# The output weights' operands made during the query projections, kept in DRAM, and loaded by the attention into eleven places

## The chip, the cores and the metric

The kernel runs on one core of a Trainium2 chip. Its time is the device time of one execution in microseconds (us). The core has five engines that run side by side and wait for one another through semaphores: PE (TensorE, the matmuls), DVE (VectorE), ACT (ScalarE), POOL (GpSimd) and SP (SyncE, which here issues most of the DMAs). Transfers that SP issues go to the DMA queue that the profile calls q1, those that POOL issues to q0.

## What is computed

A transformer block on 4 sequences of 512 tokens, 1024 wide, float32:

```python
xn = layernorm(x)                                    # (4, 512, 1024)
qkv = xn @ w_qkv                                     # 32 query heads, 8 key/value heads, 128 each
scores = q @ k.T / sqrt(128) - slope[head] * sqrt(i - j)     # causal
attn = softmax(scores) @ v
attention = attn.reshape(4, 512, 4096) @ w_o         # w_o: (4096, 1024)
ffn = xn @ W.T + b + (the rank-r product A, B of the rank that a gate picks)
out = x + attention + ffn
```

Each float32 operand is split into a high part and the remainder, and each matmul is done as three (high by high, low by high, high by low): lines 677, 678 and 679 of the kernel before.

## The kernel before

**First phase, the projections, to about 1208 us.** Two pairs of sequences, one after the other, and for each seven 1024 x 1024 weight matrices in the order values, keys, FFN, Q0, Q1, Q2, Q3. A matrix is multiplied by Strassen's and Winograd's scheme in 2 x 2 blocks, in seven steps of 48 matmuls. For each step ACT makes the high part of a weight operand (`w_hi`, line 945, two halves of 128 x 1024) and DVE the low part (`w_lo`, line 1183); sums of weight blocks (lines 1260 to 1269) and of results (`res_a`, `res_b`, `res_hi`) are DVE's too. The step's matmuls can begin on a half when its low part is there. SP loads the weight blocks (`raw<-w_all`, 1 MB each); POOL issues the stores of the results to DRAM (`qk_s`, `v_s`).

**Second phase, the attention.** 128 units (a head of one sequence each), in 8 groups of 16 units. The head changes with every unit, the sequence every four, the pair of sequences every eight and the group every sixteen. For a unit PE makes the scores (`ps<-k,q`), DVE adds the bias and finds the row maxima (`neg_max`, line 1432), ACT takes exponentials, DVE inverts the row sums (`row_inv`, line 1443, once per unit), PE transposes the probabilities (`ps<-ident,probs`, line 877), ACT and DVE split them (`pt_hi`, `pt_lo`), and PE multiplies by v.

Between these pieces PE does the output projection in "fills" (`ps<-wo,op_hi` and the like): a set of four units is multiplied by its rows of w_o, again in seven Strassen steps, for two tiles of tokens, 14 fills in a set. The set 4g is the first of group g. Its fills run in units 6 to 9 of the group, steps 0 to 3 of the first tile in unit 6 and steps 4 to 6 in unit 7. A fill's result is added to `acc` by DVE (line 1467); `acc` tiles come from and go to DRAM (`acc_s`), moved by SP.

**The operands of w_o.** Each group needs the seven Strassen operands of its own 512 rows of w_o, each as a high and a low part of 128 x 1024. Before, they are made inside the attention: SP loads four blocks `wo_raw` (line 448, 512 KB each; for a later group in unit 10 of the one before), POOL makes the four sums (`wo_sums`, line 657, in 16 pieces), ACT the seven high parts and DVE the seven low parts (`out_split`; `wo<-wo_raw` and `wo<-wo_sum` in the trace). Tables of unit numbers (WO_SUMS_IN, HIGHS_IN, LOWS_EARLY, LOWS_LAST) put all of that into units 2 to 6 of each group of 16, for the first group too; the results lie in 9 places taken in turn. In DVE's program the low parts stand after a unit's last `acc` additions, ahead of the next unit's maxima.

**SP's order at the start of the attention.** SP works through units: for unit n it issues k, q and v as needed, then the w_o loads (units 1 and 2 for the first group), then `acc` transfers. All of this is one list: a transfer that has to wait holds back those behind it.

## Time and profile before

| | us |
|---|---|
| timed, median of 3 runs | 2472.9 (2472.09 to 2473.75) |
| the profiled execution | 2475.28 |
| its span in the profile | 2473.4 |
| PE busy in the span | 2377.9 (96%) |
| DVE, ACT, POOL busy | 1547.1, 1373.4, 784.2 |
| mean granted TensorE clock | 0.991 of full speed |

Times inside the execution are counted from the start of the span. A row of the timeline gives start, duration, engine, line, operation, output<-inputs and, in brackets, how long the engine had stood idle before it and what released it. Matmuls are pipelined, so that a single one's duration is longer than the distance to the next; starts are what to read.

### The profile page before, as it was taken

How to read it: one execution, taken by the hardware profiler on the slowest of the kernel's cores; microseconds unless marked ns; L12 is line 12 of the kernel's file. 1: busy time of each engine (PE TensorE's matmuls, PEld its weight loads, DVE VectorE, ACT ScalarE, POOL GpSimd, SP SyncE). 2: the span in 40 equal slices, each digit the busy share in tenths (PEclk: the TensorE clock that was granted, in tenths of full speed). 3: DMA queues.
4: the chain of work that ended last, by engine and by line, in shares of the span. 5: the costliest groups of instructions: out<-in, count | busy, mean ns of one | idle time of the engine just before them, and what ended most of it. 6: DMA issues, size and time to landing. Idle time of an engine off the chain costs nothing.

```text
span 2473.4 us, 34303 instructions
## 1 busy us (share of the span) xinstructions
PE 2377.9 (96%) x11616; PEld 1991.7 (81%) x11616; DVE 1547.1 (63%) x2969; ACT 1373.4 (56%) x3051; POOL 784.2 (32%) x1029
## 2 busy tenths in 40 slices
PE   5999999998799999999899999999999999999999
PEld 4787888887678788888778888788888888888887
DVE  5657355655655645555676666767667666676665
ACT  4532133334533223333477777777777777777774
POOL 3211000000330100000244645446455464554644
PEclk9999999999899999999999999999999999999999
DMA  4536445546254635445655565655655556666553
GB/s 151 182 129 209 146 146 184 191 170 236 71 175 157 207 120 204 153 170 196 235 185 182 188 230 203 208 194 188 226 201 210 198 188 218 201 211 206 187 175 141
DMA packets 118318, 455.90 MB, mean 184 GB/s; under 512 B 11945, under 2 KB 12089, under 8 KB 109184
## 3 DMA queue, kind: packets, MB, share of 16 engines
q1 hardware_dynamic: 86176, 334.37, 39.2%
q0 software_dynamic: 31968, 119.33, 13.9%
q8 instruction: 94, 1.54, 0.2%
q14 instruction: 80, 0.66, 0.1%
HBM read 276.96 MB, written 176.69 MB: 183 GB/s over the span
## 4 chain that ended last, share of the span: by engine, by line
PE 85%; DVE 5%; ACT 4%; issue 3%; DMA 3%; POOL 1%; SPq 0%; ACTq 0%; DVEq 0%; POOLq 0%
PE ps L677 26%; PE ps L678 26%; PE ps L679 26%; PE ps L877 5%; DMA lora_lo<-lora_s 1%; DMA qk_s<-res_b 1%; ACT probs L1085 1%; ACT res_hi L945 1%; DVE stats L1197 1%; DVE wo L1183 1%; ACT rows L974 1%; PE ps L857 1%; ACT probs L1107 1%; DVE w_lo L1183 0%; DMA qk_s<-res_hi 0%
## 5 line engine op out<-in xcount | busy, mean ns | idle before, releaser
L945 ACT ACTIVATE w_hi<-raw 128x1024 fp32r<-128x1024 f32 x196 | 207.0, 1059 | 558.9 <-PE ps L679 439.5
L1467 DVE TENSOR_TENSOR acc<-ps,acc 128x512 f32<-128x512 f32 x448 | 297.2, 686 | 287.3 <-issue 260.8
L1183 DVE TENSOR_TENSOR w_lo<-raw,w_hi 128x1024 fp32r<-128x1024 f32 x196 | 239.1, 1224 | 357.8 <-ACT w_hi L945 357.6
L677 PE MATMUL ps<-x_hi,w_hi 128*128 128x512 f32 x1120 | 436.5, 390 | 0.0
L678 PE MATMUL ps<-x_lo,w_hi 128*128 128x512 f32 x1120 | 436.0, 389 | 0.0
L679 PE MATMUL ps<-x_hi,w_lo 128*128 128x512 f32 x1120 | 435.9, 389 | 0.0
L1085 ACT ACTIVATE probs<-probs,neg_max 128x512 f32<-128x512 f32 (+3 forms) x512 | 283.9, 566 | 168.8 <-DVE neg_max L1432 168.8
L677 PE MATMUL ps<-wo,op_hi 128*128 128x512 f32 x896 | 363.5, 406 | 2.0 <-POOL op_lo L635 0.7
L678 PE MATMUL ps<-wo,op_hi 128*128 128x512 f32 x896 | 352.1, 393 | 0.0
L679 PE MATMUL ps<-wo,op_lo 128*128 128x512 f32 x896 | 351.5, 392 | 0.0
L679 PEld LDWEIGHTS ps<-x_hi,w_lo 128*128 128x128 f32 x1120 | 210.4, 188 | 43.9
L678 PEld LDWEIGHTS ps<-x_lo,w_hi 128*128 128x128 f32 x1120 | 210.4, 188 | 43.7
L677 PEld LDWEIGHTS ps<-x_hi,w_hi 128*128 128x128 f32 x1120 | 210.5, 188 | 43.1
L561 POOL DMA_DIRECT2D qk_s<-res_hi x40 | 30.1, 753 | 652.5 <-ACT res_hi L945 634.5
L1107 ACT ACTIVATE probs<-probs,row_inv 128x128 f32<-128x128 f32 x488 | 234.3, 557 | 1.1
L1183 DVE TENSOR_TENSOR pt_lo<-ps,pt_hi 128x512 fp32r<-128x512 f32 (+1 forms) x384 | 206.8, 593 | 28.9 <-ACT pt_hi L945 28.5
L945 ACT ACTIVATE pt_hi<-ps 128x512 fp32r<-128x512 f32 (+1 forms) x384 | 173.8, 526 | 76.6 <-PE ps L877 76.6
L635 POOL TENSOR_TENSOR op_lo<-at_raw,op_hi 128x256 fp32r<-128x256 f32 x192 | 142.6, 757 | 227.6 <-ACT op_hi L945 227.6
L635 POOL TENSOR_TENSOR op_lo<-op_raw,op_hi 128x256 fp32r<-128x256 f32 x192 | 143.0, 761 | 216.9 <-ACT op_hi L945 216.3
L1432 DVE CUSTOM_DVE_ANT_0 probs<-ps,bias 128x512 f32<-128x512 f32 (+2 forms) x384 | 202.1, 551 | 3.9 <-PE ps L679 1.0
L677 PEld LDWEIGHTS ps<-wo,op_hi 128*128 128x128 f32 x896 | 169.2, 189 | 36.7 <-issue 7.8
L679 PEld LDWEIGHTS ps<-wo,op_lo 128*128 128x128 f32 x896 | 168.6, 188 | 37.4
(166 smaller groups left out, 4637.1 us busy)
## 6 DMA issues: line engine op xcount, KB each, us to landing
raw<-w_all SPq DMA_DIRECT2D x70, 1024.0 KB, 5.4
q<-qk_s SPq DMA_DIRECT2D x128, 512.0 KB, 3.9
acc<-acc_s SPq DMA_DIRECT2D x128, 512.0 KB, 5.1
acc_s<-acc SPq DMA_DIRECT2D x112, 512.0 KB, 7.7
qk_s<-res_hi POOLq DMA_DIRECT2D x40, 1024.0 KB, 4.6
qk_s<-res_a POOLq DMA_DIRECT2D x20, 1024.0 KB, 9.2
qk_s<-res_b POOLq DMA_DIRECT2D x20, 1024.0 KB, 5.2
k<-qk_s SPq DMA_DIRECT2D x32, 512.0 KB, 3.6
```

Of the source, the lines that this page charges most:

```text
L561: pool.dma_start(qk_s[b, first:first + 4, :, level, :].rearrange("h p c -> p h c"), source).then_inc(signal, 16)
L635: nc.gpsimd.tensor_tensor(op_lo[part % STEPS][:, :, :], op_source(s, part), op_hi[:, part % STEPS].bitcast(F32), ALU.subtract).then_inc(s_ ...
L677: pe.matmul(to, st_hi, mv_hi, start=start, stop=False, skip_group_check=True)
L678: pe.matmul(to, st_hi, mv_lo, start=False, stop=False, skip_group_check=True)
L679: return pe.matmul(to, st_lo, mv_hi, start=False, stop=stop, skip_group_check=True)
L877: last = pe.transpose(to[:, c * P:(c + 1) * P], probs[:, n % 2, OFF[i] + j * P:OFF[i] + (j + 1) * P], ident[:, :])
L945: nc.scalar.activation(to, source, ACT.Copy).then_inc(signal, 1)
L1085: nc.scalar.activation(tile, tile, ACT.Exp, bias=neg_max[:, i:i + 1], scale=-1.0, accum_out=row_sum[:, i:i + 1]).then_inc(s_exp, 1)
L1107: last = nc.scalar.activation(tile, tile, ACT.Copy, scale=row_inv[:, i:i + 1])
L1183: nc.vector.tensor_tensor(to, source, high.bitcast(F32), ALU.subtract).then_inc(signal, 1)
L1432: nc.vector.tensor_tensor_reduce(out=to, in0=score_bank[i], in1=added, scale=-SCALE, scalar=3e38, op0=ALU.add, op1=ALU.min, accum_out=neg_ ...
L1467: nc.vector.tensor_tensor(to, fill[f % 2][:, :], to, ALU.add).then_inc(s_acc, 1)
```

## The change

All operands of w_o are made in the first phase and written to a new DRAM tensor `wo_s`. The work is cut into 32 quarters (8 groups, each 256 of the 1024 columns) of seven operands: 224 jobs of 128 x 256, 112 in the four query matrices of each pair. A job is a high part on ACT, a low part on DVE and a store by SP of both (256 KB, in 1-KB rows) from one of four slots `wp`. The four sums of a quarter are made on DVE behind its third job. SP loads a quarter as four blocks of 128 KB. STEP_JOBS gives the number of jobs in the seven steps of a query matrix (LAST_JOBS those of Q3): half of a step's jobs stand ahead of the second half of the next weight operand on ACT and DVE, half at the step's end. ACT's high part waits until the slot's store before last use has landed. SP's stores stand in its list among the weight loads, in the order in which DVE makes them.

In the attention nothing is made. SP loads finished operands, 1 MB each in 8-KB rows, into 11 places: for group 0, steps 0 to 3 in unit 1 and 4 to 6 in unit 2; for later groups steps 0 to 3 in units 10 to 13 of the group before and steps 4 to 6 in unit 6 of its own. PE waits for the load where it waited for the low part. The `bias` tile moves by 10 KB. POOL's `wo_sums`, the tables and the making are gone.

```diff
+QUARTERS = 4 * KV_HEADS
+JOBS = QUARTERS * STEPS
+WO_ORDER = (6, 1, 0, 4, 2, 5, 3)
+STEP_JOBS = (3, 5, 4, 5, 5, 4, 4)
+LAST_JOBS = (3, 5, 4, 5, 4, 2, 0)
+SLOTS = 4
+WO_PLACES = 11
...
+            def quarter(c, i):
+                group, part = c // 4, c % 4
+                head = group * G + 2 * (i % 2) + part // 2
+                first = (i // 2) * 512 + (part % 2) * 256
+                sp.dma_start(wp_raw[i][:, :], w_o[bass.ds(head * P, P), first:first + 256]).then_inc(s_wp_raw[i], 16)
+
+            def operands_out(pr, m, st, part_=None):
+                if m == Q0 and st == 0:
+                    sp.wait_ge(s_bank, 4 * (number(pr, FFN, STEPS - 1) + 1))
+                    for i in range(4):
+                        quarter(pr * QUARTERS // PAIRS, i)
+                for j in jobs(pr, m, st, part_):
+                    c, i = j // STEPS, j % STEPS
+                    part = slice(c % 4 * 256, (c % 4 + 1) * 256)
+                    sp.wait_ge(s_wp_lo, j + 1)
+                    sp.dma_start(wo_s[c // 4, WO_ORDER[i], :, :, part], wp[:, j % SLOTS].bitcast(F32)
+                                 ).then_inc(s_wp_out[j % SLOTS], 16)
+                    if i >= 3 and (c + 1) % (QUARTERS // PAIRS):
+                        sp.wait_ge(s_wp_sum, 4 * (c + 1))
+                        quarter(c + 1, {3: 2, 4: 3, 5: 1, 6: 0}[i])
...
+            def out_operand(group, step):
+                if used(group, step) is not None:
+                    sp.wait_ge(s_fill, used(group, step))
+                sp.dma_start(wo[wo_place(group, step)][:, :, :].bitcast(F32), wo_s[group, step]).then_inc(s_wo[step], 16)
 
             def out_weights(n):
                 if n in (1, 2):
-                    sp.wait_ge(s_bank, 4 * TOTAL)
-                    for i in ((0, 2), (1, 3))[n - 1]:
-                        out_block(0, i)
...
+                    if n == 1:
+                        sp.wait_ge(s_bank, 4 * TOTAL)
+                        operands_are_out(JOBS)
+                    for step in (range(0, 4), range(4, STEPS))[n - 1]:
+                        out_operand(0, step)
+                group, since = n // GROUP_UNITS, n % GROUP_UNITS
+                if since == 6 and group:
+                    for step in range(4, STEPS):
+                        out_operand(group, step)
+                if since in range(10, 14) and group + 1 < GROUPS:
+                    out_operand(group + 1, since - 10)
...
+            def job(j):
+                c, step = j // STEPS, WO_ORDER[j % STEPS]
+                if j >= SLOTS:
+                    act.wait_ge(s_wp_out[j % SLOTS], 16 * (j // SLOTS))
...
+                high(wp[:, j % SLOTS, 0], wp_source(step), s_wp_hi)
...
+            def job(j):
+                c, i = j // STEPS, j % STEPS
+                dve.wait_ge(s_wp_hi, j + 1)
...
+                low(wp[:, j % SLOTS, 1], wp_source(WO_ORDER[i]), wp[:, j % SLOTS, 0], s_wp_lo)
+                if i != 2:
+                    return
...
+                nc.vector.tensor_tensor(a21, a11, a21, ALU.subtract).then_inc(s_wp_sum, 1)
...
                         later_operand(pr, m, st, 1)
+                        for j in jobs(pr, m, st, 0):
+                            job(j)
                         weights(n + 1, 1)
...
                         ahead(pr, m, st)
+                        for j in jobs(pr, m, st, 1):
+                            job(j)
...
-                for part in making(n, LOWS_EARLY):
-                    out_split(*part)
...
-                for part in making(n, LOWS_LAST):
-                    out_split(*part)
```

How the order of instructions changes at three places. First DVE's list in unit 4 of a group (the first group change), before; `wo` is a low part of an operand, `acc` the addition of a fill, the ISA rows are the maxima of the next unit:

```order
L1443 RECIPROCAL row_inv<-row_sum 128x4
L1467 TENSOR_TENSOR acc<-ps,acc 128x512 x3
L1183 TENSOR_TENSOR wo<-wo_raw_93,wo 128x1024
L1183 TENSOR_TENSOR wo<-wo_raw_96,wo 128x1024
L1432 ISA probs,neg_max<-ps,bias 128x512
```

The same place after:

```order
L1463 RECIPROCAL row_inv<-row_sum 128x4
L1487 TENSOR_TENSOR acc<-ps,acc 128x512 x3
L1452 ISA probs,neg_max<-ps,bias 128x512
L1452 ISA neg_max 128x1
L1452 ISA probs,neg_max<-ps,bias 128x384
```

The two low parts between the last addition and the next maxima are gone; so are those of units 2, 5 and 6. Second, SP's list at the start of the attention, before, from the load of unit 1's q to that of unit 4's:

```order
L513 DMA q<-qk_s 128x1024
L448 DMA wo_raw_93<-w_o 128x2x512
L448 DMA wo_raw_95<-w_o 128x2x512
L513 DMA q<-qk_s 128x1024
L448 DMA wo_raw_94<-w_o 128x2x512
L448 DMA wo_raw_96<-w_o 128x2x512
L513 DMA q<-qk_s 128x1024
L474 DMA acc<-acc_s 128x1024 x2
L512 DMA k<-qk_s 128x1024
L513 DMA q<-qk_s 128x1024
```

And after:

```order
L554 DMA q<-qk_s 128x1024
L489 DMA wo_107<-wo_s 128x2048
L489 DMA wo_108<-wo_s 128x2048
L489 DMA wo_109<-wo_s 128x2048
L489 DMA wo_110<-wo_s 128x2048
L554 DMA q<-qk_s 128x1024
L489 DMA wo_111<-wo_s 128x2048
L489 DMA wo_112<-wo_s 128x2048
L489 DMA wo_113<-wo_s 128x2048
L554 DMA q<-qk_s 128x1024
L515 DMA acc<-acc_s 128x1024 x2
```

Ahead of unit 2's q stand four transfers of 1 MB where two of 512 KB stood, and three more of 1 MB ahead of unit 3's. Third, DVE's list where the matrix Q1 of the first pair ends and Q2 begins, before; `res_b` are the results of Q1's last step, lines 1260 to 1265 the sums of weight blocks for Q2:

```order
L1183 TENSOR_TENSOR res_b<-ps,res_hi 128x512 x4
L1183 TENSOR_TENSOR w_lo<-raw_55,w_hi 128x1024
L1260 TENSOR_TENSOR raw_57<-raw_56,raw_57 128x2048
L1262 TENSOR_TENSOR raw_56<-raw_54,raw_56 128x2048
L1265 TENSOR_TENSOR raw_54<-raw_57,raw_54 128x2048
L1183 TENSOR_TENSOR w_lo<-raw_54,w_hi 128x1024
```

And after, where `wp` is the low part of a job:

```order
L1203 TENSOR_TENSOR res_b<-ps,res_hi 128x512 x4
L1203 TENSOR_TENSOR wp<-wp_raw_78,wp 128x256
L1203 TENSOR_TENSOR wp<-wp_raw_76,wp 128x256
L1203 TENSOR_TENSOR w_lo<-raw_55,w_hi 128x1024
L1280 TENSOR_TENSOR raw_57<-raw_56,raw_57 128x2048
L1282 TENSOR_TENSOR raw_56<-raw_54,raw_56 128x2048
L1285 TENSOR_TENSOR raw_54<-raw_57,raw_54 128x2048
L1203 TENSOR_TENSOR wp<-wp_raw_75,wp 128x256
L1203 TENSOR_TENSOR w_lo<-raw_54,w_hi 128x1024
```

Two jobs stand ahead of the first weight half and one ahead of the second. Where Q0 ends and Q1 begins it is two jobs with a quarter's four sums between them.

## Rows read from the trace of the kernel before

**Rows 1.** Page, part 4: what the chain that ended last consists of, by engine.

```profile
PE 85%; DVE 5%; ACT 4%; issue 3%; DMA 3%; POOL 1%; SPq 0%; ACTq 0%; DVEq 0%; POOLq 0%
```

**Rows 2.** Windows: length, busy us (instructions) by engine, PEclk, DMA share, GB/s.

```profile
378.00:454.00 76.00, 76.00 (x337) 62.94 (x336) 42.31 (x37) 27.94 (x33) 6.03 (x8) 1.00 0.51 179
...
1352.00:1508.00 156.00, 153.34 (x816) 130.84 (x815) 106.01 (x275) 118.17 (x318) 78.14 (x104) 0.99 0.59 202
...
1215.00:1220.00 5.00, 4.39 (x17) 4.10 (x17) 3.84 (x13) 1.02 (x4) 1.11 (x2) 0.52 1.03 411
```

**Rows 3.** Timeline of DVE: the inverted row sums of units 16, 32, 48, 56 and 64.

```profile
1352.02 0.18 DVE L1443 RECIPROCAL row_inv<-row_sum 128x4 f32<-128x4 f32 x1 [0.60 <-ACT probs L1085]
...
1508.49 0.18 DVE L1443 RECIPROCAL row_inv<-row_sum 128x4 f32<-128x4 f32 x1 [0.60 <-ACT probs L1085]
...
1663.77 0.18 DVE L1443 RECIPROCAL row_inv<-row_sum 128x4 f32<-128x4 f32 x1 [0.60 <-ACT probs L1085]
...
1743.40 0.18 DVE L1443 RECIPROCAL row_inv<-row_sum 128x4 f32<-128x4 f32 x1 [0.60 <-ACT probs L1085]
...
1819.03 0.18 DVE L1443 RECIPROCAL row_inv<-row_sum 128x4 f32<-128x4 f32 x1 [0.61 <-ACT probs L1085]
```

**Rows 4.** Timeline of DVE in unit 4 of the fourth group.

```profile
1707.03 0.69 DVE L1467 TENSOR_TENSOR acc<-ps,acc 128x512 f32<-128x512 f32 x1 [3.68 <-issue]
1707.64 3.45 DVE L1183 TENSOR_TENSOR wo<-wo_raw,wo 128x1024 fp32r<-128x1024 f32 x2
1711.01 0.68 DVE L1432 CUSTOM_DVE_ANT_0 probs<-ps,bias 128x512 f32<-128x512 f32 x1
```

**Rows 5.** What PE waited for, 1250 us to the end: us, times, longest.

```profile
PE ps L877 <- DVE neg_max L1432: 19.1, 15, 1.8
```

**Rows 6.** Timeline of SP at the start of the attention: issues.

```profile
1208.07 0.90 SPq L448 DMA_DIRECT2D wo_raw<-w_o  x2
...
1210.83 0.47 SPq L513 DMA_DIRECT2D q<-qk_s  x1
...
1226.10 0.43 SPq L513 DMA_DIRECT2D q<-qk_s  x1
```

**Rows 7.** Timeline of PE: the first matmul of the scores of units 2, 3, 4 and 7.

```profile
1215.61 0.80 PE L677 MATMUL ps<-k,q 128*128 128x512 f32 x1 [3.13 <-DMA q<-qk_s]
...
1226.05 0.39 PE L677 MATMUL ps<-k,q 128*128 128x512 f32 x1
...
1233.00 0.47 PE L677 MATMUL ps<-k,q 128*128 128x512 f32 x1 [3.90 <-DMA q<-qk_s]
...
1262.65 0.39 PE L677 MATMUL ps<-k,q 128*128 128x512 f32 x1
```

**Rows 8.** DMA queues from 1213 to 1224: packets, MB, share of 16 engines.

```profile
q1 hardware_dynamic: 799, 1.97, 49.9%
q0 software_dynamic: 543, 2.10, 46.6%
```

**Rows 9.** Timeline of DVE where Q1 of the first pair ends and Q2 begins.

```profile
457.95 2.48 DVE L1183 TENSOR_TENSOR res_b<-ps,res_hi 128x512 f32<-128x512 f32 x4 [1.40 <-DMA qk_s<-res_b]
...
470.10 1.23 DVE L1183 TENSOR_TENSOR w_lo<-raw,w_hi 128x1024 fp32r<-128x1024 f32 x1 [1.19 <-ACT w_hi L945]
```

**Rows 10.** Timeline of PE: the first matmul of the step that needs that `w_lo`.

```profile
475.79 0.39 PE L677 MATMUL ps<-x_hi,w_hi 128*128 128x512 f32 x1
```

**Rows 11.** Lines by form: ns min/median/max of a 128 x 256 operation on ACT and DVE.

```profile
L945 ACT ACTIVATE op_hi<-at_raw x192: 401/413/426, 1248.2 to 2461.3; 128x256 fp32r<-128x256 f32 x192
...
L1405 DVE TENSOR_TENSOR d_mask<-u_mask x2: 424/424/425, 200.6 to 800.0; 128x256 f32<-128x256 f32 x2
```

**Rows 12.** DMA issues: count, KB each, median us from issue to landing.

```profile
qk_s<-res_hi POOLq DMA_DIRECT2D x40, 1024.0 KB, 4.6
...
v_s<-res_hi POOLq DMA_DIRECT2D x32, 256.0 KB, 3.7
```

**Rows 13.** Timeline of DVE near the end of the first pair's Q3.

```profile
589.18 1.23 DVE L1183 TENSOR_TENSOR w_lo<-raw,w_hi 128x1024 fp32r<-128x1024 f32 x1 [3.39 <-ACT w_hi L945]
```

More of the change, by code:

```diff
@@ L117, in block_program @@
         d_lo = at("d_lo", 192 * K + 10624, [P, 512], F32R)
+        wp_raw = [at(f"wp_raw{i}", (192 + i) * K, [P, 256]) for i in range(4)]
+        wp = at("wp", 196 * K, [P, SLOTS, 2, 256], F32R)
         rest = 192 * K + 12800
@@ L434, in _ @@
                             tokens(pr + 1, 1)
+                    operands_out(pr, m, 3, 1)
+                    operands_out(pr, m, 4, 0)
+                    if follow is not None:
                         sp.wait_ge(s_w_lo, split(number(pr, m, 5), 1))
@@ L438, in _ @@
                             tokens(pr + 1, 2)
+                    operands_out(pr, m, 4, 1)
+                    operands_out(pr, m, 5, 0)
+                    if follow is not None:
                         sp.wait_ge(s_w_lo, split(number(pr, m, 6), 1))
@@ L669, in _ @@
                     out_low(s, part)
-                for group, step in making(n, WO_SUMS_IN):
-                    wo_sums(group, step)
         @block.tensor
@@ L1169, in _ @@
                     normalise(n)
-                for part in making(n, HIGHS_IN):
-                    out_split(*part)
         @block.vector
@@ L1500, in _ @@
                         later_operand(pr, m, st, 1)
+                        for j in jobs(pr, m, st, 0):
+                            job(j)
                         weights(n + 1, 1)
@@ L1505, in _ @@
                         ahead(pr, m, st)
+                        for j in jobs(pr, m, st, 1):
+                            job(j)
                 leave(number(pr, MATRICES - 1, STEPS - 1))
@@ L1520, in _ @@
                     add_fill(*f)
-                for part in making(n, LOWS_LAST):
-                    out_split(*part)
 def constants():
```

134 lines of the change are left out of this document (54 added, 80 removed).

## The prediction

> **What bounds the kernel now.** I read the chain that ended last first: 85% of it is PE [rows 1]. So only time that PE stands idle can be won, and other engines count where they hold PE up. The windows say where that is: in a query matrix PE is busy for all 76.00 us of 76 [rows 2], with DVE at 42.31 and ACT at 27.94; in a group of the attention it is busy 153.34 of 156. The inverted row sums, one for each unit, are the clock of the attention. Units 56 to 64 take 1819.03 - 1743.40 = 75.63 us, or 9.45 a unit; a group at that pace would take 151.26. Units 48 to 64 take 155.26 and units 16 to 32 take 156.47 [rows 3]. A group change therefore costs 4.0 us, the first one 5.2. The timeline shows why: in unit 4 DVE starts two low parts `wo` at 1707.64, 3.45 us together, and the next maxima start only behind them at 1711.01 [rows 4]. PE's list of waits over the attention names the same thing: 19.1 us in 15 waits for `neg_max` [rows 5]. The rest of the 29.2 is matmuls that run slower right after such a wait. At the attention's start PE waits twice for a q, 3.13 and 3.90 us [rows 7], while the transfers run at 411 GB/s and the granted clock is 0.52, the lower of the two levels for nearly all of the stretch [rows 2].
>
> **What goes: the making inside the attention.** The seven changes of group after the first cost 6 x 4.0 + 5.2 = 29.2 us. With `wo` off DVE, what is late next? DVE stood idle 3.68 us before the `acc` addition ahead of those low parts [rows 4], so the maxima would follow that addition at about 1707.6 and be done well before PE's transposes came to wait. I know of no second wait there, and in the eight units without making PE runs at 9.45 throughout. So the whole goes: **-29.2**. The bound from the other side is the waits alone, -19.1, if the slower matmuls have another cause. ACT's seven high parts and POOL's sums at those places hid behind PE and give nothing.
>
> **What comes in the steady attention: loads.** 56 loads of 1 MB where 32 of 512 KB stood: +42 MB over some 1220 us, +34 GB/s on 202 [rows 2], of the 411 that the start shows. Steps 0 to 3 have five to nine units' time before their fill. Steps 4 to 6 are issued in SP's unit 6; SP runs ahead of PE and gets there when PE's fills of unit 4 have freed the places, and the fill of step 4 comes in unit 7. That is about two units, 18.9 us, for 3.1 MB, which take 7.7 us alone and some 15 beside 202 GB/s of other transfers. Queued behind them is q of unit 7, with a unit and a half to spare. **0**.
>
> **What comes at the attention's start.** Before, 1.05 MB of w_o stood ahead of unit 2's q and 2.10 MB ahead of unit 3's; now 4.19 and 7.34 MB. The stretch is already full, each queue with half of the engines' time [rows 8]. From SP's issues at 1208 to 1211 [rows 6] the bytes ahead of unit 2's q, itself included, are 4.7 MB. If q1 had the full 411 GB/s it would land at 1220.5; with half of it until the stores of q0 end near 1225, at 1228. I take 1225, against 1215.6: PE is late by 9.4. For unit 3's q the split does not matter: 7.34 + 1.05 MB and 2.3 MB of stores make 10.7 MB, 26 us, so it lands at 1235, when PE, 9.4 late, comes for it (1226.05 + 9.4 = 1235.5). Unit 4's q is issued behind `acc` and k (2.1 MB more, 5.1 us): 1240.5, against 1233.00 [rows 7], so 8 late. Then it is made good in part: the group-0 making, seven low parts of 1.2 us on DVE and as many high parts on ACT, stood in just these units 2 to 6, and the chain of units 4 to 7 (1233.00 to 1262.65, 29.7 us where steady units take 28.4) ran partly through it. I keep **+5**, between -2 (the lateness swallowed, the making's waits gone) and +10 (nothing made good).
>
> The Trainium skill, "DMA: Bandwidth & Descriptors", section Specifications, gives about 358 GB/s as what one core gets from the memory, and the row shows 411 in a stretch of loads and stores together, so the trace doesn't agree. By 358 unit 3's q would land about 4 us later, and the time would be some 2456; the sum goes by the row.
>
> **What comes in the projections: 224 jobs.** A job is 0.41 on ACT and 0.42 on DVE, and a quarter's sums 4 x 0.42 [rows 11]. A query matrix has 28 to 30 jobs: 12 us on ACT, and 12.6 + 4.3 x 1.7 = 20 us on DVE. Both have the room: 27.94 + 12 and 42.31 + 20 of 76 [rows 2]. What matters is where they stand. The tightest place of a matrix is the first half of step 2's `w_lo`: it ends at 470.10 + 1.23 = 471.33 and PE needs it at 475.79, a slack of 4.5 [rows 9, 10]. Ahead of it now stand two jobs and one more, 1.3 us, or, where Q0 ends, two jobs with the four sums and one more, 2.9, part of it inside waits that DVE has anyway (1.40 and 1.19 us, rows 9). That fits. A job can also come late because its slot's store has not landed: then ACT waits, and what queues behind is `w_hi` and so `w_lo`. A slot comes round after four jobs, which is about one step of 10.9 us, at the closest some 5; a store of 256 KB to DRAM lands in 3.7 us [rows 12]. That leaves 1 to 2 us of slip at the worst places, still within 4.5. For what I did not see, **+1.5**, from 0 to 6.
>
> Each pair's stores and quarter loads are 37.7 MB in 1-KB runs on a queue that has 0.51 of the engines' time busy in a query matrix [rows 2]. Nothing in this trace has such runs. At 25 GB/s for each of 16 engines a run takes 41 ns; q1's 799 packets of 1.97 MB in 11 us at 49.9% took 110 ns each for 2.5 KB [rows 8], and a straight line down to 1 KB, drawn through q0's 151 ns for 3.9 KB, gives about 68. So 36,900 runs over 305 us cost 0.31 to 0.51 of the engines: 0.82 to 1.02 in all. I take 55 ns, 0.93. This is the least known of the numbers.
>
> Between the pairs, in Q3 of the first, DVE and ACT are late by themselves: DVE waits 3.39 us for ACT's `w_hi` at 589.18 [rows 13]. Three jobs stand in that part, 2 x 0.41 + 0.42: **+1.3**, from 0.4 (hidden but one) to 3. In the second pair's Q3, SP gets to unit 0's k, q and v only behind the last store of the projections, some 30 us later than before but still ahead of the attention: **+0.5**, 0 to 3.
>
> **The sum** on the profiled span: 2473.4 - 29.2 + 5 + 1.5 + 1.3 + 0.5 = 2452.5. The profiled execution took 2475.28 with its span of 2473.4, and the median of the timed runs is 2472.9, half a us under the span. So **2452**.
>
> **Rivals.**
> - *Projections held up by the stores (slower).* If engines at 0.93 let stores land not after 3.7 but 10 us or more, four slots no longer cover a step. ACT waits for a slot, `w_hi` and `w_lo` come late, and beyond the slack of 4.5 PE pays one us for each us in each of the eight query matrices. The gain is used up when step 2's `w_lo` is 4.5 + 20.9/8 = 7.1 us late; at 8 late, 3.5 x 8 = 28 on 2452: 2480. For it: the share above, and 1-KB runs. Against it: the weight loads' room (0.51 is a mean, with pauses) and that POOL's four stores of 256 KB in a row each land in 3.7 us [rows 12], so small stores overlap. The Trainium skill, "DMA: Bandwidth & Descriptors", section Rules for kernel authors, asks for at least 1 MiB in one DMA for the full rate; the rows agree in direction (1 MB in 4.6 us, 256 KB in 3.7), and the change goes against it. Chance 0.10.
> - *The gain is half eaten.* A start late by 10 that stays, or group changes that keep the third that is not in the list of waits (29.2 - 19.1 = 10): 2460 to 2468, chance 0.12. Both together, or 1 MB loads that make a q late at each of the seven changes by 3 us (+21): 2468 to 2478, which is no change; 0.06. The last is the case in which the change does not do what it says: PE waits at the group change as before, for DMA instead of DVE.
> - *The start costs nothing*, and the projections neither: 2438 to 2444, chance 0.10.
>
> **How the numbers follow.** The forecast, 2452 with a range of its own of 2444 to 2460 (start -2 to +10, projections 0 to 6, which do not all fall to one side), has 0.62. Faster by over 0.2% (5 us, about what a measurement here can tell from no change) is below 2468: 0.62 + 0.12 + 0.10 = 0.84. Within 0.2%: 0.06. Slower: 0.10. From 2438 to 2468 lie 0.84, and that is the range.
>
> **What would show it.** Right: 16 units of the attention take 151.3 us in every group, with no `neg_max` waits at a group change; query matrices still take 76.2 us; the scores of units 2 to 4 wait for q until about 1225 to 1241 and unit 7's begin some 5 us later than 1262.65; a store `wo_s<-wp` lands in 4 to 7 us. Wrong: waits of PE on `w_lo` in query matrices behind an ACT that waits for `wo_s`; waits of the fills on `wo<-wo_s`, or of the scores on q, in units 6 and 7 of each group; an attention phase that begins later than 1208 + 3.

## The result, and the profile after

The changed kernel takes 2563.0 us (median of 4, 2560.62 to 2565.55); the kernel before takes 2472.55 beside it (2472.09 to 2473.75). The ratio is 1.0365, interval 1.0347 to 1.0383: slower by 90 us, where 2452 was forecast and 2468 was the range's end.

The first row to look for is the one that parts the two phases: the inverted row sums of the attention's first unit, on DVE's timeline. In the kernel before:

```profile
1209.39 0.17 DVE L1443 RECIPROCAL row_inv<-row_sum 128x4 f32<-128x4 f32 x1
```

After (units 0, 16 and 32):

```profile
1318.31 0.17 DVE L1463 RECIPROCAL row_inv<-row_sum 128x4 f32<-128x4 f32 x1
...
1466.84 0.18 DVE L1463 RECIPROCAL row_inv<-row_sum 128x4 f32<-128x4 f32 x1 [0.60 <-ACT probs L1102]
...
1618.10 0.18 DVE L1463 RECIPROCAL row_inv<-row_sum 128x4 f32<-128x4 f32 x1 [0.60 <-ACT probs L1102]
```

Unit 0 comes 108.9 us later. Units 16 to 32, the first whole group behind a group change, take 1618.10 - 1466.84 = 151.26 us, where [rows 3] has 156.47. So the attention did what was forecast, and the projections lost four times as much as it won. The spans: 108.9 (projections) + 5.9 (the first 16 units, 148.5 against 142.6) - 29.2 (seven group changes) = +85.6, and the spans differ by 2558.8 - 2473.4 = 85.4.

Where in the projections? The windows (length, busy us and instructions of PE, PEld, DVE, ACT, POOL, granted clock, DMA share, GB/s) over the whole stretch in which the first pair's four query matrices run. In the kernel before, the stretch is 326 us long and holds 1378 matmuls:

```profile
301.00:627.00 326.00, 312.61 (x1378) 259.31 (x1377) 183.69 (x190) 123.18 (x148) 24.72 (x33) 0.98 0.51 181
```

After, the same 1378 matmuls take 383.5 us. The second line is the matrix window of [rows 2], the third the 76 us behind it:

```profile
301.00:684.50 383.50, 330.12 (x1378) 266.68 (x1377) 246.74 (x366) 159.89 (x260) 24.72 (x33) 0.94 0.74 252
...
378.00:454.00 76.00, 64.69 (x260) 51.47 (x259) 44.42 (x62) 29.40 (x52) 4.51 (x6) 0.93 0.74 250
454.00:530.00 76.00, 67.92 (x288) 55.06 (x287) 52.05 (x70) 31.32 (x51) 6.03 (x8) 0.96 0.79 265
```

PE is idle for 53.4 us instead of 13.4, and its matmuls take 17.5 us longer in all, with the mean granted clock at 0.94 instead of 0.98. The idle time is the greater part of the loss; the lower clock beside it goes with some 13 of the 17.5 (312.6 x 0.98 / 0.94 = 325.9, an estimate). DVE and ACT are far from full (247 and 160 of 383.5), and the DMA engines stand at 0.74. None of them is used up over this stretch; something waits. What ACT waited for in this stretch (us, times, longest):

```profile
ACT wp L962 <- DMA wp_raw<-w_o: 93.6, 31, 7.4
...
ACT wp L962 <- DVE wp_raw L1500: 14.2, 10, 2.8
ACT wp L962 <- DMA wo_s<-wp: 13.9, 7, 6.3
```

ACT stands for 93.6 us at 31 jobs whose quarter block has not landed. Its timeline shows who is queued behind such a job:

```profile
385.18 0.42 ACT L962 ACTIVATE wp<-wp_raw 128x256 fp32r<-128x256 f32 x1 [1.95 <-DMA wp_raw<-w_o]
391.38 0.42 ACT L962 ACTIVATE wp<-wp_raw 128x256 fp32r<-128x256 f32 x1 [5.78 <-DMA wp_raw<-w_o]
391.71 1.04 ACT L962 ACTIVATE w_hi<-raw 128x1024 fp32r<-128x1024 f32 x1
```

`w_hi` at 391.71 is the next weight operand of PE. It needs nothing of the job, but ACT works its list in order, so it starts 5.78 us late. The chain that ended last shows the whole loop (start, us, what):

```profile
411.31 0.77 DVE wp L1203 x2
...
412.31 0.61 SPq L413
...
412.96 0.51 SPq L425
...
413.52 3.83 DMA wp_raw<-w_o
...
417.44 0.43 ACT wp L962
...
417.88 0.43 DVE wp L1203
418.31 0.35 DVE wp_raw L1500
...
419.98 1.13 DVE w_lo L1203
```

A job's low part on DVE (411.31) frees a block; SP issues loads and the store between them; the load takes 3.83; only then come the next high part, the low part, the quarter's sums, and behind those the `w_lo` that PE waits for. This pass takes 8.7 us, and a half step of PE is about 5.4. Before, DMA had 3% of the chain by engine [rows 1]; the page after:

```profile
PE 69%; DVE 11%; DMA 9%; ACT 5%; issue 3%; SPq 2%; POOL 1%; DVEq 0%; ACTq 0%; POOLq 0%
```

### The profile page after: what moved, and what is told of

It reads as the page before. It is cut to its first block, busy times and chain, and to the rows that moved or that the text cites. A ratio compares the mean times of both kernels' runs of the same rounds, so it can differ in the third digit from the quotient of the medians.

```text
span 2558.8 us, 35298 instructions
## 1 busy us (share of the span) xinstructions
PE 2403.8 (94%) x11616; PEld 2008.9 (79%) x11616; DVE 1606.1 (63%) x3265; ACT 1395.1 (55%) x3219; POOL 663.4 (26%) x901
## 3 DMA queue, kind: packets, MB, share of 16 engines
q0 software_dynamic: 31968, 119.33, 13.4%
## 4 chain that ended last, share of the span: by engine, by line
PE 69%; DVE 11%; DMA 9%; ACT 5%; issue 3%; SPq 2%; POOL 1%; DVEq 0%; ACTq 0%; POOLq 0%
PE ps L694 21%; PE ps L695 21%; PE ps L696 21%; DMA wp_raw<-w_o 5%; PE ps L894 5%; DVE w_lo L1203 2%; ACT res_hi L962 1%; DVE wp L1203 1%; ACT w_hi L962 1%; DVE res_a L1293 1%; SPq L425 1%; DMA wo_s<-wp 1%; SPq L413 1%; DMA qk_s<-res_b 1%; DVE res_a L1203 1%
## 5 line engine op out<-in xcount | busy, mean ns | idle before, releaser
L694 PE MATMUL ps<-x_hi,w_hi 128*128 128x512 f32 x1120 | 451.0, 403 | 63.8 <-DVE w_lo L1203 54.5
L695 PE MATMUL ps<-x_lo,w_hi 128*128 128x512 f32 x1120 | 445.0, 397 | 0.0
L696 PE MATMUL ps<-x_hi,w_lo 128*128 128x512 f32 x1120 | 444.2, 397 | 0.0
L696 PEld LDWEIGHTS ps<-x_hi,w_lo 128*128 128x128 f32 x1120 | 215.8, 193 | 46.7
L695 PEld LDWEIGHTS ps<-x_lo,w_hi 128*128 128x128 f32 x1120 | 216.5, 193 | 44.6
L962 ACT ACTIVATE wp<-wp_raw 128x256 fp32r<-128x256 f32 x224 | 88.6, 416 | 237.6 <-DMA wp_raw<-w_o 177.7
```

The lines of the kernel that those rows point to most:

```text
L694: pe.matmul(to, st_hi, mv_hi, start=start, stop=False, skip_group_check=True)
L695: pe.matmul(to, st_hi, mv_lo, start=False, stop=False, skip_group_check=True)
L696: return pe.matmul(to, st_lo, mv_hi, start=False, stop=stop, skip_group_check=True)
L962: nc.scalar.activation(to, source, ACT.Copy).then_inc(signal, 1)
```

## The experiments

Theories: (1) the quarter loads, each issued behind the job that frees its block and wanted three jobs later, hold ACT up; (2) the four slots come round before their stores have landed, the prediction's rival; (3) the added transfers crowd the DMA engines, so that everything lands later; (4) the jobs' own work on ACT and DVE is too much. The measure is the time of unit 0's row sums, which leaves out what the attention wins.

| kernel | time, us | unit 0, us | over before |
|---|---|---|---|
| before | 2472.55 | 1209.4 | |
| after | 2563.0 | 1318.3 | 108.9 |
| e1: no later quarter loads | 2496.78 | 1256.2 | 46.8 |
| e2: no later stores | 2484.78 | 1242.0 | 32.6 |
| e6: neither | 2458.88 | 1215.0 | 5.6 |
| e21: both issued, nobody waits | 2479.43 | 1236.5 | 27.1 |
| e3: six blocks, loaded earlier | 2514.57 | 1273.5 | 64.1 |
| e14: best form of the change found | 2482.67 | 1246.1 | 36.7 |
| e19: making kept, DVE's order changed | 2448.62 | 1209.4 | 0.0 |

e1, e2, e6, e7, e9, e12, e13 and e21 are single runs; the others have 4 or 5, with an interval. Each was timed beside its own runs of the kernel before, whose medians lie between 2471.96 and 2476.11; the ratios go by those. The times of unit 0 are those of the profiled executions:

```profile
1256.21 0.17 DVE L1460 RECIPROCAL row_inv<-row_sum 128x4 f32<-128x4 f32 x1
...
1242.03 0.17 DVE L1466 RECIPROCAL row_inv<-row_sum 128x4 f32<-128x4 f32 x1
...
1215.01 0.17 DVE L1463 RECIPROCAL row_inv<-row_sum 128x4 f32<-128x4 f32 x1
...
1236.48 0.17 DVE L1488 RECIPROCAL row_inv<-row_sum 128x4 f32<-128x4 f32 x1
```

These are e1, e2, e6 and e21. The four leave out transfers that the result needs, or send them elsewhere; they serve for the time alone.

**Taking the transfers away: e1, e2, e6.** In e1 the quarter loads behind a pair's first quarter go:

```diff
-                    if i >= 3 and (c + 1) % (QUARTERS // PAIRS):
-                        sp.wait_ge(s_wp_sum, 4 * (c + 1))
-                        quarter(c + 1, {3: 2, 4: 3, 5: 1, 6: 0}[i])
```

> Leaves out the loads of w_o quarters after the first of each pair (every job works on the same four blocks, so the operands are wrong); all jobs, sums and stores stay. Theory A (ACT waits for the 128 KB quarter load, whose block comes free only three jobs before it is needed, and w_hi queues behind that wait): the 109 us that the changed kernel is late at the first unit nearly vanish, query matrices back to 76 to 78 us, time 2450 to 2465. Theory B (stores in 1-KB runs crowd the DMA engines and land late, slots not free): 16 MB of some 75 MB are gone, so at least 80 of the 109 stay, 2530 or more. Theory C (the jobs' own work on ACT and DVE, and where it stands, holds w_hi and w_lo up): no change, about 2555.

In e2 the stores of groups 1 to 7 go, and with them ACT's wait for their landing:

```diff
-                    sp.dma_start(wo_s[c // 4, WO_ORDER[i], :, :, part], wp[:, j % SLOTS].bitcast(F32)
...
+                    if c < 4:
+                        sp.dma_start(wo_s[c // 4, WO_ORDER[i], :, :, part], wp[:, j % SLOTS].bitcast(F32)
...
```

> Leaves out the stores of the operands of groups 1 to 7 (the attention loads group 0's every time, so the result is wrong); jobs and quarter loads stay. Theory A: the waits for quarter loads stay, though each load lands sooner than 5.9 us and SP issues it sooner: from Q1 of the first pair on the matrices still take 82 to 92 us, time 2490 to 2545. Theory B: matrices back to 76 to 78 us, time 2450 to 2465. Theory C: about 2555.

e6 is both edits together.

> Leaves out both the quarter loads after the first of each pair and the stores of groups 1 to 7 (result wrong); the jobs' work on ACT and DVE stays, in its places. e1 brought the changed kernel from 2563 to 2497, e2 to 2485. If waits for transfers (A and B together) are all of the loss: query matrices 76.2, time 2440 to 2450. If the jobs' own work in its places (C) is the rest: Q1 and Q2 stay at 77 to 80 us each and Q3 of the first pair above 100, time 2455 to 2475.

Over e6, the loads alone cost 1242.0 - 1215.0 = 27 us, the stores alone 41, and both 103. Together they cost more than the sum; they share a loop and a queue, but no run shows which of the two makes the difference. e1 and e2 met none of the ranges set for them: each range took one cause to be nearly all. In each half-kernel ACT waits for the one kind that is left. ACT's waits from 300 to 640, e1:

```profile
ACT wp L959 <- DMA wo_s<-wp: 58.8, 22, 6.3
```

and e2:

```profile
ACT wp L964 <- DMA wp_raw<-w_o: 59.4, 19, 6.2
```

So (1) and (2) are both real; in the changed kernel the loads come last and hide the slots. e6 has all 224 jobs on ACT and DVE, and its first matrix windows read:

```profile
378.00:454.00 76.00, 74.58 (x330) 61.32 (x329) 59.01 (x86) 37.48 (x64) 6.24 (x9) 1.00 0.54 193
454.00:530.00 76.00, 76.00 (x337) 62.94 (x336) 58.12 (x84) 35.90 (x60) 5.81 (x8) 1.00 0.51 179
```

DVE is at 58 to 59 us of 76, and PE is full in the second window as it was in [rows 2]. The work itself costs at most 5.6 us in all (group 0's transfers are still in e6); (4) is out as the main cause. The time of e6 lies in the range forecast for this case, that the jobs' own work leaves a rest (2455 to 2475).

**The traffic without the waits: e21.** e6 with the same number of loads and stores issued in the same places of SP's list, but into two blocks that no job reads and from a slot that no job waits for:

```diff
+                    if c >= 4 and not 0 <= j - JOBS // PAIRS < SLOTS:
+                        sp.dma_start(wo_s[c // 4, WO_ORDER[i], :, :, part], wp[:, 3].bitcast(F32)).then_inc(s_idle_out, 16)
...
+                        if turn_:
+                            sp.wait_ge(s_idle_in[home], 16 * turn_)
...
+                        sp.dma_start(idle[home][:, :], w_o[bass.ds(head * P, P), first:first + 256]).then_inc(s_idle_in[home], 16)
```

SP itself still waits, before a load, for the one that went into the same block before (73 us in 35 waits, 45 us of it in the first pair), and group 0's real stores stand behind these waits in its list.

> As e6 (jobs work on blocks that stay, result wrong), with the transfers put back for which nobody waits: SP issues a store of 256 KB in 1 KB runs for each job, from a slot that does not change, and a 128 KB load into a block that no job reads, in the places of the real ones. If the transfers cost only through what waits for them: within 6 us of e6's 2459. If they slow the weight loads and result stores by themselves (crowding): 2475 or more, with PE waiting for w_lo behind raw loads.

It took 20.6 us more than e6, which is the outcome set for crowding (2475 or more). The windows of 301 to 606, e6:

```profile
301.00:606.00 305.00, 299.73 (x1321) 247.43 (x1319) 230.94 (x341) 146.39 (x244) 21.84 (x29) 1.00 0.59 206
```

and e21:

```profile
301.00:606.00 305.00, 295.02 (x1283) 240.84 (x1282) 220.75 (x322) 141.96 (x238) 20.32 (x27) 0.99 0.82 281
```

The DMA engines stand at 0.82, and the transfers land later. DMA issues from 301 to 640 (count, KB each, median us to landing), e6:

```profile
raw<-w_all SPq DMA_DIRECT2D x20, 1024.0 KB, 6.2
...
qk_s<-res_hi POOLq DMA_DIRECT2D x16, 1024.0 KB, 4.6
```

and e21:

```profile
wo_s<-wp SPq DMA_DIRECT2D x112, 256.0 KB, 6.7
raw<-w_all SPq DMA_DIRECT2D x20, 1024.0 KB, 8.5
qk_s<-res_hi POOLq DMA_DIRECT2D x15, 1024.0 KB, 6.4
```

The way in which that costs is not the forecast one: in the changed kernel and in e21 no engine waits for a weight block `raw<-w_all`. What is waited for longer in e21 is the stores of the projections' own results: DVE for `qk_s<-res_b` 25.7 us, in e6 10.1, and ACT for `qk_s<-res_hi` 21.5, in e6 3.0 (both pairs).

So (3) has a share, but a bounded one. In the second pair e21 loses 6.6 us on e6; in the first it is 14.9, in part because the jobs of group 0, which are real in both kernels, wait there for their stores. Crowding by itself is therefore at most about 21 of the 109 us; how much of the 21 is due to SP's own waits in e21 is not shown. The other 82 come only when somebody waits for the added transfers: ACT with `w_hi` behind, and the lower clock that goes with PE's pauses.

**Mending the loads: e3, and the start: e4.** e3 has six quarter blocks in rotation, so that each load is issued at least five jobs before its use:

```diff
-        wp_raw = [at(f"wp_raw{i}", (192 + i) * K, [P, 256]) for i in range(4)]
+        wp_raw = [at(f"wp_raw{i}", place_, [P, 256])
+                  for i, place_ in enumerate((192 * K, 193 * K, 194 * K, 195 * K, 204 * K, rest + 1664))]
...
+                    ahead_, role = {3: (1, 0), 4: (1, 2), 5: (2, 3), 6: (2, 1)}.get(i, (99, 0))
...
-                        quarter(c + 1, {3: 2, 4: 3, 5: 1, 6: 0}[i])
+                        quarter(c + ahead_, role)
```

> The whole change, with six blocks for quarters in place of four, taken in turn, so that every block is loaded five jobs or more before it is needed; same transfers, same stores, same jobs. Theory A: query matrices 76 to 79 us, first unit some 100 us earlier than in the changed kernel, time 2450 to 2470, faster than before. Theory B or C: within 15 us of the changed kernel's 2563.

2514.57, ratio 1.0164 [1.0149, 1.0179]: 48 us of the 90 are back, which meets neither range. The waits for loads are all but gone (4.8 us in both pairs), and the slots have taken their place. ACT's waits of e3, 300 to 640:

```profile
ACT wp L981 <- DMA wo_s<-wp: 74.4, 30, 7.2
```

The Trainium skill, "DMA: Bandwidth & Descriptors", section Rules for kernel authors, says to issue a DMA early and wait on its semaphore late; the loads of e3 agree. The slots show the other side: a ring of four places is only as early as its fourth job back. In e3 a slot is held for some 8.8 us (median over the 224 jobs, from the start of its high part on ACT to the landing of its store, worked out from the times in the trace), and 6.0 of these are the landing.

e4 also spreads the loads of group 0:

```diff
-                if n in (1, 2):
+                if n in range(1, 7):
...
-                    for step in (range(0, 4), range(4, STEPS))[n - 1]:
+                    for step in ((0,), (1,), (2,), (3,), (4,), (5, 6))[n - 1]:
```

> As e3, and group 0's operands are loaded one in each of units 1 to 5 and two in unit 6 instead of four in unit 1 and three in unit 2, so that no more stands ahead of the first q loads than before the change. If the 7 MB ahead of q cost what the prediction's step said (5 us), this is 4 to 8 us faster than e3: the scores of unit 2 begin within 1 us of where they would after the projections' end plus 7.5, those of unit 7 about 5 us sooner. Rival: the start is bound by the projections' last stores and acc loads, and nothing changes (0 to 1 us).

2506.92, ratio 1.0139 [1.0122, 1.0156], 7.65 less than e3, as forecast. The row sums show where most of it is: group 0's sixteen units take 1421.38 - 1273.54 = 147.8 in e3 and 1412.75 - 1271.05 = 141.7 in e4. The kernel before has 142.6, so the seven transfers in a bunch were the start's whole cost, and spreading them takes it away.

**Another spread of the jobs: e9, e7.** Instead of 3 and 5 jobs in the first two steps of a matrix, 4 and 4:

```diff
-STEP_JOBS = (3, 5, 4, 5, 5, 4, 4)
-LAST_JOBS = (3, 5, 4, 5, 4, 2, 0)
+STEP_JOBS = (4, 4, 4, 5, 5, 4, 4)
+LAST_JOBS = (4, 4, 4, 4, 4, 2, 0)
```

e9 is the changed kernel with that, e7 is e3 with that.

> The changed kernel with its four blocks and only the even spread of e7. If the wait for quarter loads is the first cause by itself (a block is needed again three jobs after it came free, however the jobs are spread): 2540 to 2563. If the slots are the first cause: below 2525.

> As e3 (six blocks, all transfers), with the jobs spread more evenly over a matrix: 4, 4, 4, 5, 5, 4, 4 in its steps in place of 3, 5, 4, 5, 5, 4, 4, so that a slot is seldom asked for again within 5.4 us. Theory B2 (what is left in e3 is ACT waiting for a slot, 74 us of waits in the first pair, because five jobs in a step go through four slots and a store takes 6 us to land): those waits fall below 40 us and the time to 2480 to 2500. If the evenness does not matter: 2510 to 2518.

e9 2555.91, e7 2509.94: 5 to 7 us better in one run each, but the waits stay, 107.3 us for loads in e9 (to 660) and 73.3 us for slots in e7. e9 fell where the loads as first cause had put it. That e7's slot waits would fall below 40 was wrong: to spread the steps with five jobs does not shorten them.

**The slots: e11 to e14.** e11 is e7 with e4's start and with the jobs of a matrix's first step all at that step's end (`half = (len(mine) + 1) // 2 if st else 0`).

> e7, with the jobs of a matrix's first step all at the step's end (none ahead of the weight operand and the weight sums that the tightest place of the matrix hangs on) and with group 0's loads spread as in e4. Expected: query matrices 76 to 79 us, time 2450 to 2470, faster than before. If the first step's jobs do not matter: e7's time less the 6 to 8 us of e4.

2501.08, ratio 1.0116 [1.0099, 1.0133]; slot waits 75.0 us in 36. The forecast of 2450 to 2470 failed; what came is e7's time less 9, about the gain of e4's start, so that the first step's jobs hardly matter. e12 is e11 with the stores issued by POOL, on q0, out of SP's list:

```diff
-                    sp.wait_ge(s_wp_lo, j + 1)
-                    sp.dma_start(wo_s[c // 4, WO_ORDER[i], :, :, part], wp[:, j % SLOTS].bitcast(F32)
+                    pool.wait_ge(s_wp_lo, j + 1)
+                    pool.dma_start(wo_s[c // 4, WO_ORDER[i], :, :, part], wp[:, j % SLOTS].bitcast(F32)
...
```

> As e11 (six blocks, even spread, spread start; 2501 us), with the stores of the operands issued by POOL on q0 in place of SP on q1; SP keeps the quarter loads, which no longer stand behind a store. If slots come free late because a store stands in SP's list and in q1 behind 1 MB weight loads: ACT's waits for wo_s in the first pair fall from 75 us to below 30, Q1 and Q2 to 76 to 80 us, time 2460 to 2480. If they are late because the DMA engines are crowded by 1-KB runs, whichever queue holds them: within 10 us of 2501.

e13 is e11 with 2-KB runs, each quarter of an operand in one piece of DRAM:

```diff
-        wo_s = nc.dram_tensor("wo_s", (KV_HEADS, STEPS, P, 2, 1024), F32).ap()
+        wo_s = nc.dram_tensor("wo_s", (KV_HEADS, STEPS, 4, P, 2, 256), F32).ap()
```

> As e11, with wo_s laid out so that a job's store is in runs of 2 KB in place of 1 KB (and the attention's loads in runs of 2 KB in place of 8). Theory B (the count of small runs crowds the DMA engines): half the packets, stores land in 4 to 5 us instead of 6.1, and the time falls to 2465 to 2490. If the queue's order is what makes them late: 2495 to 2505.

e14 is both.

> e12 and e13 together. With both theories true in part it is the fastest so far, 2455 to 2470, and faster than before; if neither: 2490 to 2505.

e12 2492.54, e13 2496.64, e14 2482.67 with ratio 1.0041 [1.0027, 1.0056]. e12 fell where crowding had put it and e13 where the queue's order had: each speaks against the theory that it was built for, and e14 lies between its two ranges. What did not move is the landing: a store takes 6.1 us in e11, 6.6 in e12, 6.1 in e13, 6.5 in e14, whichever queue and whichever run length. What it goes with shows when the 224 stores of a kernel are sorted by whether a 1-MB transfer (`raw<-w_all`, `qk_s<-res_hi`, `res_a` or `res_b`) is on its way when they are issued. In the changed kernel the 70 without one land in 2.5 us (median) and the 154 with one in 6.3; in e14 it is 75 in 3.3 and 149 in 7.5. ACT's waits for slots fall only from 75.0 to 58.0. What e14 wins over e11, 18.4 us, is more than the two edits alone (8.5 and 4.4), and no run settles by which way. It is still slower than before.

**The jobs on POOL: e15 to e18.** POOL is nearly idle in the projections. In e15 (e7 with e4's start) it does all of a job: high part by `tensor_copy`, low part, sums; ACT and DVE have none.

```diff
+                nc.gpsimd.tensor_copy(wp[:, j % SLOTS, 0], wp_source(c, step)).then_inc(s_wp_hi, 1)
+                nc.gpsimd.tensor_tensor(wp[:, j % SLOTS, 1], wp_source(c, step), wp[:, j % SLOTS, 0].bitcast(F32),
+                                        ALU.subtract).then_inc(s_wp_lo, 1)
```

> Six blocks, even spread and spread start as in e11 (without its move in the first step), with every job, high part, low part and sums, on POOL, which does 6 of 76 us in a query matrix. The same transfers from the same queue, so the same waits for slots, but only POOL waits, and no weight operand is queued behind it. If the loss is that ACT's wait for a slot or a block holds up w_hi: query matrices 76.2 to 77 us, time 2440 to 2455, faster than before by 1%. If the transfers themselves hold the projections up (weight blocks that land late, 7.4 us for 5.4): 2475 or more. A third way: POOL, some 60 us of work in a matrix of 76, is late with the stores of results and holds up ACT's and DVE's leaving: 2460 to 2500.

e16 is e15 with 2-KB runs.

> e15 with wo_s in runs of 2 KB (as e13). If e15 is free of waits in the projections, the run length matters nowhere: within 4 us of e15. If POOL is late for its slots: 3 to 10 us faster than e15.

2533.09, ratio 1.0232 [1.0214, 1.0251], and 2533.17, ratio 1.0241 [1.0226, 1.0256]. No weight operand waits behind a job any more, but POOL also issues the stores of the projections' results, and now those stand behind jobs. ACT's waits in e15, 300 to 680:

```profile
ACT res_hi L1013 <- DMA qk_s<-res_hi: 65.5, 6, 19.7
```

The wait has moved from one engine's list to another's, which was the third of the ways set down, at a higher price than its 2460 to 2500. e16 did not move, as forecast for run lengths that do not matter, though POOL does wait for its slots (33.5 us in e15). Moreover a job is dear on POOL where DVE sums weight blocks (the last section has the rows).

e17 divides: POOL takes two of a quarter's seven jobs, with a slot and stores of its own, ACT and DVE take five with three slots; 2-KB runs, spread start, STEP_JOBS (2, 4, 5, 5, 5, 5, 4).

```diff
+        def by_pool(j):
+            return j % STEPS >= 5
...
+            return 3 if by_pool(j) else turn_of(j) % 3
```

> Two of the seven jobs of a quarter (the last two sums' operands) on POOL with a slot of their own and their stores on q0, the other five on ACT and DVE with three slots, which come round every 11 us of a matrix in place of every 9; six blocks, 2 KB runs, spread start; 2 jobs in a matrix's first step. If a job's wait costs because w_hi queues behind it, and fewer and longer turns end most of the waits: query matrices 76 to 78 us, time 2445 to 2462, faster than before. If POOL's share again makes the stores of results late: 2465 to 2490. If the bytes are what counts: 2478 or more.

e18 is e17 with STEP_JOBS (4, 4, 4, 5, 5, 4, 4).

> e17 with 4, 4, 4, 5, 5, 4, 4 jobs in the steps of a matrix in place of 2, 4, 5, 5, 5, 5, 4. If the jobs at the head of a matrix are what is left (work ahead of the tightest weight operand): 3 to 10 us slower than e17; if slots are: 0 to 4 us faster.

2500.87, ratio 1.0114 [1.0099, 1.0129], and 2497.88, ratio 1.0099 [1.0082, 1.0116]: no better than e14, and the two are the same within the noise. In e17 the three slots still cost ACT 44.3 us of waits and the single one POOL 111.1. The time lies in the range set for the bytes (2478 or more), but with the slots waiting it does not show them to be the cause. In none of the forms that ran do four slots suffice; more than four were not tried.

**The gain without the change: e19, e20.** The prediction put the group changes' 29.2 us down to where DVE's low parts stand [rows 4]. If so, it is the place that costs, not the making. e19 is the kernel before, making and all, with the low parts of units 4 and 6 (table rows 8 and 10; row k is unit k - 4) ahead of a unit's last addition of a fill, and that of unit 5 (row 9) moved into unit 6:

```diff
-LOWS_EARLY = {9: (2,), 10: (4,)}
-LOWS_LAST = {6: (1,), 8: (0, 6), 9: (3,), 10: (5,)}
+LOWS_EARLY = {9: (2,), 10: (3,)}
+LOWS_MID = {8: (0, 6), 10: (4,)}
+LOWS_LAST = {6: (1,), 10: (5,)}
...
-                for f in todo[1:]:
+                for f in todo[1:-1]:
                     add_fill(*f)
+                for part in making(n, LOWS_MID):
+                    out_split(*part)
+                for f in todo[1:][-1:]:
+                    add_fill(*f)
```

> The kernel before, everything made in the attention as before, with the low parts of w_o in another place of DVE's list: those of steps 0 and 6 in unit 4, and of step 4, ahead of the unit's last acc addition, in the 2.9 to 3.7 us in which DVE stands idle there; step 3 a unit later in the place of step 4, so that none stands at the end of unit 5. If the loss at a group change is only DVE's order ahead of the maxima, as the reading of the rows said: each change of group costs 0 to 1 us instead of 4.0, time 2444 to 2455, faster than before. If the making as such (ports, ACT, POOL) costs it: 2468 to 2474.

e20 moves only the two of unit 4 (row 8).

> As e19 with only the two low parts of unit 4 moved. The reading says that PE's two waits in a group change are one behind each place (0.75 and 1.81 us, with slower matmuls after them): 2455 to 2466, between before and e19.

e19: 2448.62 (2447.93 to 2449.39), ratio 0.9891 [0.9874, 0.9907], faster than both kernels. e20: 2461.24, ratio 0.9941 [0.9926, 0.9956]. Both lie in their ranges. DVE's timeline of e19 at the place of [rows 4]:

```profile
1696.79 3.03 DVE L1184 TENSOR_TENSOR wo<-wo_raw,wo 128x1024 fp32r<-128x1024 f32 x2 [2.29 <-ACT wo L946]
1699.75 0.68 DVE L1468 TENSOR_TENSOR acc<-ps,acc 128x512 f32<-128x512 f32 x1
1700.35 0.68 DVE L1433 CUSTOM_DVE_ANT_0 probs<-ps,bias 128x512 f32<-128x512 f32 x1
```

The two low parts now run while the last fill is still on PE, where DVE stood idle before, and the maxima follow the addition at once. What PE waited for from 1250 us to the end, where [rows 5] had 19.1 us for `neg_max`, is four items in e19, of which these are the longest two:

```profile
PE ps L678 <- issue: 2.4, 7, 0.4
PE ps L878 <- DVE probs L1449: 0.7, 1, 0.7
```

A group takes 151.9 instead of 155.3, against 151.26 without any making: the loss at a group change is 0.6 instead of 4.0. In e20 it is 2.2, with groups of 153.5.

## Why the prediction was wrong

- **The group changes, -29.2: right.** Every group behind a change takes 151.25 or 151.26 us, the 9.45 a unit that was worked out. e19 shows the cause as well: with the low parts elsewhere in DVE's list, all but 0.6 of the 4.0 goes, so the slower matmuls behind the waits belonged to them too, and the lower bound of 19.1 was too low.
- **Loads in the steady attention, 0: right.** PE's waits after, from 1330 to the end, name no weight operand, and no q beyond the start's two; the longest two of four items:

```profile
PE ps L694 <- DMA q<-qk_s: 14.9, 2, 11.8
PE ps L694 <- DVE pt_lo L1203: 5.1, 3, 1.8
```

- **The start, +5: right, 5.9.** The scores of units 2, 3, 4 and 7 after, on PE's timeline:

```profile
1334.17 0.80 PE L694 MATMUL ps<-k,q 128*128 128x512 f32 x1 [11.76 <-DMA q<-qk_s]
...
1344.18 0.40 PE L694 MATMUL ps<-k,q 128*128 128x512 f32 x1
...
1350.38 0.47 PE L694 MATMUL ps<-k,q 128*128 128x512 f32 x1 [3.14 <-DMA q<-qk_s]
...
1377.49 0.39 PE L694 MATMUL ps<-k,q 128*128 128x512 f32 x1
```

Less 108.9 they are 1225.3, 1235.3, 1241.5 and 1268.6; 1225, 1235.5 and 1240.5 were forecast for the first three, and the last is 5.9 later than in [rows 7]. The rate of 411 GB/s from the rows fitted: 403 GB/s stood from 1317 to 1347. The 358 GB/s of the Trainium skill, "DMA: Bandwidth & Descriptors", section Specifications, did not. What was missed is that the loads need not stand in a bunch (e4).

- **The jobs in the projections: the step that failed.** The three terms in it (1.5 for the jobs, 1.3 between the pairs, 0.5 in the second pair's Q3) made +3.3; they measured +108.9. It failed in three places.
  - First, the quarter loads were priced only as bytes, in the share of the DMA engines. That each load is issued by SP after a job on DVE and wanted three jobs later was in the diff (`quarter` behind `s_wp_sum`), and no line of the working gives it a wait; these waits came to 93.6 us of ACT in one pair, and taking them away (e3) gave 45 of the 109 back.
  - Second, a slot was given "about one step of 10.9 us, at the closest some 5", against 3.7 us for a store. The store takes 5.3 (median of all 224), 6.3 with a 1-MB transfer on its way, and before it come ACT's part, DVE's place in its own list and SP's place in its list; in e3, where the slots come last, that makes some 8.8 us in all. The row taken for the landing, POOL's `v_s` stores in [rows 12], is mostly of stores with nothing large beside them: 24 of its 32 were issued with no 1-MB transfer on its way and landed in 3.5, the other eight in 4.1. What brings 4.1 to 6.3 is not shown.
  - Third, 1 to 2 us of slip were set against a slack of 4.5 as if each wait stood alone. A job that starts late frees its block and its slot late, so the next turn of the loop begins from there: 31 waits in one pair, one for every three or four jobs, and ten of them (4.7 to 7.4 us) are longer than the slack even alone.
- **The DMA share: about right, and not the point.** 55 ns was taken for a 1-KB run, between 41 and 68. The queue q1 (packets, MB, share of 16 engines) from 301 to 640, e6:

```profile
q1 hardware_dynamic: 12224, 33.03, 28.4%
```

and e21:

```profile
q1 hardware_dynamic: 43712, 62.93, 56.7%
```

  The 31,488 packets more took 28.3% of 16 x 339 us: 49 ns each. The share reached 0.82, not 0.93. It was watched as the thing that decides, and what decided was the time of one small transfer in a loop, which had risen to 6.3 us behind a 1-MB transfer while the share stood at 0.74.
- **The rival** named the mechanism, ACT waiting with `w_hi` and `w_lo` behind, and the direction. But its condition (stores that land after 10 us or more) did not come about (4 of the 224 did), it had the slots where the loads came last, and its price was one late `w_lo` per matrix, 28 us in all. Its evidence against, POOL's stores at 3.7 us, came mostly from stores with nothing large beside them.
- **Between the pairs, +1.3:** Q3 of the first pair went from 97.1 to 115.7 us. In e6, with the jobs and without their later transfers, it takes 97.9, so that the jobs' own work there costs some 0.8, within 0.4 to 3; the rest comes with those transfers. By the tables Q3 has 22 jobs and the other three matrices 30, where the working says 28 to 30; no term hangs on it.

What stays open is how the 109 us divide. Crowding is 21 at most and the jobs' own work 5.6 at most; the loads and the slots cannot be parted, since each hides the other.

## What to carry to other kernels

Before work is moved into another phase, walk once round every loop that it brings (place free, transfer issued, landed, used, place free again), with the landing time under that phase's load, and look at what stands behind the waiting instruction in its engine's list: a spare engine is no cover for work that waits there ahead of the critical operand. And when work costs time at one place, first ask whether it is the work or its place in the list: here a few lines of reordering won 27 us (e19, 2448.6 beside 2476.1) with all of the work left in its phase.

## What had not been expected of the hardware

In e15, POOL's operations on 128 x 256 slow down by more than three times while DVE adds blocks of weights. POOL's timeline, then DVE's over the same time:

```profile
394.54 2.67 POOL L639 TENSOR_TENSOR wp<-wp_raw,wp 128x256 fp32r<-128x256 f32 x1
397.17 2.78 POOL L645 TENSOR_TENSOR wp_raw<-wp_raw,wp_raw 128x256 f32<-128x256 f32 x1
400.09 2.60 POOL L648 TENSOR_TENSOR wp_raw<-wp_raw,wp_raw 128x256 f32<-128x256 f32 x1
402.77 0.74 POOL L650 TENSOR_TENSOR wp_raw<-wp_raw,wp_raw 128x256 f32<-128x256 f32 x1
```

```profile
394.04 2.57 DVE L1316 TENSOR_TENSOR raw<-raw,raw 128x2048 f32<-128x2048 f32 x1
396.64 2.71 DVE L1318 TENSOR_TENSOR raw<-raw,raw 128x2048 f32<-128x2048 f32 x1
399.46 2.64 DVE L1321 TENSOR_TENSOR raw<-raw,raw 128x2048 f32<-128x2048 f32 x1
```

Each of the three long POOL operations ends some 0.6 us behind the DVE sum beside it, as if it had run only then; the same form takes 0.74 once DVE has done. DVE's sums take 2.57 to 2.71. The Trainium skill, "SBUF — State Buffer", section Who interferes with whom, says that a DVE instruction with two SBUF inputs contends with a GpSimd instruction that reads SBUF; these rows agree. DVE pays too: the same sums take 2.28 us in the changed kernel, where POOL has no such work.

The landing time of a 256-KB store was the other surprise: 3.7 us in [rows 12], 5.2 to 6.5 over the first phase (medians) in the kernels whose jobs are on ACT and DVE alone, hardly changed by the queue or by runs of 2 KB instead of 1. The median hides two kinds, 2.5 and 6.3 in the changed kernel, and which it is goes with whether a 1-MB transfer is on its way.
